# One f32 TanH per decoding step, read twice: its upper half as bf16, the whole of it as f32 weights

## The reference

```python
def step(carry, tgt):
    s, c, alpha = carry
    f = conv(alpha, conv_w)
    e = einsum('a,bta->bt', va, tanh(enc_proj + (s @ Wa_s.T)[:, None, :] + f @ Wa_f.T + ba))
    e = where(mask, e, -1e30)
    alpha_new = softmax(e, axis=1)
    g = einsum('bt,btd->bd', alpha_new, hbatch)
    y = tanh(g @ L_gy_w.T + L_gy_b + s @ L_sy.T) @ L_yy_w.T + L_yy_b
    rec = tgt @ L_ys.T + s @ L_ss.T + g @ L_gs_w.T + L_gs_b
    ig, fg, cg, og = split(rec, 4, axis=1)
    c_next = sig(fg) * c + sig(ig) * tanh(cg)
    s_next = sig(og) * tanh(c_next)
    return (s_next, c_next, alpha_new), y
```

## Time and profile before

| what | us |
|---|---|
| median of 3 runs | 1757.52 |
| the runs | 1752.98, 1757.52, 1757.66 |
| profiled execution, its own time | 1752.67 |
| span of the profiled execution | 1750.9 |
| PE busy | 1652.3 |
| DVE busy | 926.0 |
| ACT busy | 526.4 |
| POOL busy | 385.6 |

### The profile page before, as it was taken

One profiled execution on the slowest core, in us unless ns is written; L12 is line 12 of the kernel. 1 busy time (PEld: TensorE's weight loads), 2 busy tenths in 40 slices (PEclk: granted clock), 3 DMA queues, 4 the chain that ended last, 5 costly groups with the idle time before them and its releaser, 6 DMA issues.

```text
span 1750.9 us, 47280 instructions
## 1 busy us (share of the span) xinstructions
PE 1652.3 (94%) x17747; PEld 960.1 (55%) x17747; DVE 926.0 (53%) x4293; ACT 526.4 (30%) x2023; POOL 385.6 (22%) x1030
## 2 busy tenths in 40 slices
PE   5557999999999999999999999999999999997999
PEld 3444454544555566666666666666666666663443
DVE  5996643331455555555555555555555555553422
ACT  1442230320333333333333333333333333331211
POOL 3334321220000122222222222222222222222311
PEclk8558999999999999999999999999999999997999
DMA  8430000000300000000000000000000000000000
GB/s 323 166 106 8 1 1 0 1 1 9 123 0 0 0 0 0 0 0 0 0 0 0 0 0 0 0 0 0 0 0 0 0 0 0 0 0 1 1 25 25
DMA packets 17363, 34.51 MB, mean 20 GB/s; under 512 B 7476, under 2 KB 8675, under 8 KB 17332
## 3 DMA queue, kind: packets, MB, share of 16 engines
q1 hardware_dynamic: 17332, 34.10, 5.4%
HBM read 32.00 MB, written 2.10 MB: 19 GB/s over the span
## 4 chain that ended last, share of the span: by engine, by line
PE 88%; DVE 8%; issue 2%; POOL 1%; ACT 1%; SPq 1%; DMA 0%; POOLq 0%; DVEq 0%; ACTq 0%
PE bank L1188 27%; PE bank L1073 11%; PE bank L1256 10%; PE bank L1088 6%; PE bank L1232 5%; PE bank L1200 4%; PE bank L1184 4%; PE bank L1206 3%; PE bank L1214 2%; PE bank L1242 2%; PE bank L1219 2%; PE bank L1178 2%; PE bank L1054 1%; DVE xn L559 1%; DVE smax L609 1%
## 5 line engine op out<-in xcount | busy, mean ns | idle before, releaser
L1188 PE MATMUL bank<-krep,identb 128*128 128x512 f16 (+1 forms) x2048 | 604.8, 373 | 0.0
L1256 PE MATMUL bank<-krep,uh 128*128 128x128 f32 x1024 | 215.8, 323 | 0.4 <-DVE krep L764 0.4
L1256 PEld LDWEIGHTS bank<-krep,uh 128*128 128x128 f32 x1024 | 150.0, 188 | 107.8 <-DVE krep L764 91.0
L493 POOL TENSOR_TENSOR sscale<-ex,rinv 128x8 f32 x256 | 50.7, 198 | 645.5 <-DVE rinv L755 645.5
L1188 PEld LDWEIGHTS bank<-krep,identb 128*128 128x128 bf16 x2048 | 171.0, 97 | 8.1
L764 DVE TENSOR_TENSOR krep<-inv,ahn 128x128 f32<-128x128 f32 x512 | 162.3, 356 | 0.0
L1073 PE MATMUL bank<-xT,wbig 128*128 128x512 f16 x672 | 158.2, 387 | 3.6 <-DVE xT L591 3.6
L963 ACT ACTIVATE xs<-gat 64x8 f32<-64x8 f32 x256 | 53.1, 207 | 285.9 <-DVE gat L771 285.9
L743 DVE TENSOR_TENSOR rs<-bank,rin 128x8 f32<-128x8 f32 x256 | 42.7, 167 | 177.5 <-PE bank L1206 177.5
L955 ACT ACTIVATE interT<-bank 128x128 f16<-128x128 f32 x256 | 70.9, 277 | 200.7 <-PE bank L1200 200.7
L1232 PEld LDWEIGHTS bank<-eh,krep 128*128 128x128 f16 x2048 | 67.7, 96 | 102.3 <-ACT eh L960 102.3
(11 more groups left out here) (205 smaller groups left out, 3150.9 us busy)
## 6 DMA issues: line engine op xcount, KB each, us to landing
wbig<-d_gate_qT SPq DMA_DIRECT2D x4, 896.0 KB, 10.0
wbig<-d_up_qT SPq DMA_DIRECT2D x4, 896.0 KB, 20.8
wbig<-d_down_qT SPq DMA_DIRECT2D x1, 3584.0 KB, 30.6
d_out<-x_sb SPq DMA_DIRECT2D x8, 256.0 KB, 2.0
sscale<-d_gate_sT SPq DMA_DIRECT2D x2, 896.0 KB, 8.5
interT<-d_gate_sT SPq DMA_DIRECT2D x2, 896.0 KB, 14.9
sscale<-d_up_sT SPq DMA_DIRECT2D x2, 896.0 KB, 4.2
interT<-d_up_sT SPq DMA_DIRECT2D x2, 896.0 KB, 4.2
```

The source lines that it names most:

```text
L1188: mm(bank[1][:, 0:n], identb[:], hg2[:, 0].rearrange("p h g -> p (h g)")[:, 0:n], start=True, stop=True)
L1256: mm(bank[0][:, 0:P], uh[:, h, :], qv[:, h, :, :], start=False, stop=False, skip_group_check=True)
```

## The change

- ScalarE makes the TanH once, in f32, into `th`, and signals `th_full`. The f16 version and its semaphore are gone.
- The row scores (L1214 before, L1207 after) read `th_top`: the upper 16 bits of each f32 word of `th`, taken as bf16, so every second 16-bit element.
- The column scores are one f32 matmul (L1211 after): `th` as weights, `vae` (8 columns, f32) as moving data. VectorE's subtraction (L746) is gone, and so are the matmul with the remainder (L1222) and its wait.
- The filler ahead of the row scores has 512 columns in place of 384; the filler between L1219 and L1222 is gone. So seven fillers of 512 columns are left.
- In the setup the two VectorE operations that made `vae2` are gone.

```diff
-        vae2 = sb("vae2", [P, 2, 2 * B], F16)
-        th_hi = interT[:, 6, P:P + P // 2].bitcast(F16)
-        th_lo = interT[:, 6, 2 * P:2 * P + P // 2].bitcast(F16)
+        th_top = th.bitcast(BF16).rearrange("p (n two) -> p two n", two=2)[:, 1, :]
...
-            in_halves(vae2[:], vae[:].rearrange("p h b -> p (h b)"))
...
-                    dve.wait_ge(s["th_full"], l + 1)
-                    nc.vector.tensor_tensor(th_lo, th, th_hi, ALU.subtract).then_inc(s["th_lo_ready"], 1)
...
-                    nc.scalar.activation(th_hi, bank[0][:, 0:P], ACT.Tanh).then_inc(s["th_s"], 1)
                     nc.scalar.activation(th, bank[0][:, 0:P], ACT.Tanh).then_inc(s["th_full"], 1)
...
-                    keep_busy(384)
-                    pe.wait_ge(s["th_s"], l + 1)
+                    keep_busy(512)
+                    pe.wait_ge(s["th_full"], l + 1)
                     for b in range(B):
                         for h in range(2):
-                            last = mm(bank[2][b * TH:(b + 1) * TH, h * TH:(h + 1) * TH], vah[:, h, :], th_hi[:, b * TH:(b + 1) * TH],
+                            last = mm(bank[2][b * TH:(b + 1) * TH, h * TH:(h + 1) * TH], vah[:, h, :], th_top[:, b * TH:(b + 1) * TH],
                                       start=False, stop=True, skip_group_check=True)
                     last.then_inc(s["eb_done"], 1)
 
-                    for j in range(2):
-                        mm(bank[3][:, 0:8], th_hi, vae2[:, j, :], start=False, stop=False, skip_group_check=True)
-                    keep_busy(512)
-                    pe.wait_ge(s["th_lo_ready"], l + 1)
-                    mm(bank[3][:, 0:8], th_lo, vae2[:, 0, :], start=False, stop=True, skip_group_check=True).then_inc(s["et_done"], 1)
+                    mm(bank[3][:, 0:8], th, vae[:].rearrange("p h b -> p (h b)"), start=False, stop=True, skip_group_check=True).then_inc(s["et_done"], 1)
 
                     keep_busy(512)
                     keep_busy(512)
```

More of the change, by code:

```diff
@@ L264, in build @@
             vbd_zero setup_v setup_mm setup_cp mask_ready scale_ready
-            pre_done th_s th_full th_lo_ready eb_done et_done mx_ready eh_ready ex_ready el_ready sum_done ah_done hg_done rinv_ready ahn_ready
+            pre_done th_full eb_done et_done mx_ready eh_ready ex_ready el_ready sum_done ah_done hg_done rinv_ready ahn_ready
             prod_ready g_ready q0_ready q1_ready kept tg_ready ab_ready c_ready tc_ready s_ready sh_ready sl_ready sp_done
@@ L1171, in _ @@
             pe.wait_ge(s["rin_ready"], 2 * B)
-            pe.wait_ge(s["part_ready"], 5)
+            pe.wait_ge(s["part_ready"], 4)
             pe.wait_ge(s["identb_ready"], 1)
```

## The result

The changed kernel takes 1760.13 us (median of 20 runs) against 1756.95 us for the one before (20 runs): ratio 1.0021, 95% interval 1.0011 to 1.0031, so 1.9 to 5.4 us slower. The forecast was 1.3 us less. The time lies in the stated range and within 0.3% of the forecast, but it moved the other way, and by more than its interval leaves open. The prediction took 0.3% as the least that such runs can tell; 20 runs of each kernel tell 0.2%.

A forecast was written before the change was run, and what follows sets the result against it. The column scores' path to the exponential was taken to bound each step; 0.05 of filler and 0.39 of f32 matmul nearly replaced it, -0.005 us a step, -1.3 us over 256, giving 1756.2 us, range 1741 to 1768.

The forecast's parts named there:

- the first rival: Filler doesn't hold the row scores' weights: -0.06 us a step, 1742 us; chance 0.15 together with a cheaper f32 matmul.
- Point 1: Filler ahead of the row scores, 384 to 512 columns: their weights load 0.05 us later each step.
- Point 2: Row scores reading every second 16-bit element: no cost, with 0.06 us a step as upper bound.
- Point 3: Column scores' weights can load at 1003.75, which is 1003.70 plus the filler's 0.05 us.
- Point 4: Column scores' f32 matmul, from first load to last end: 0.39 us, with bounds of 0.22 and 0.49.
- the second rival: Column scores' f32 matmul costs more than its columns, full 0.49 us: +0.09 a step, 1780 us; chance 0.12.
- the third: Strided row scores read at half rate: at most +0.06 us a step, 1771 us; chance 0.05.
- Point 6: VectorE's maximum of the row scores: ready at 1004.09, with 0.05 us to spare before the column scores.
- Point 7: Exponential starts at 1004.18 against 1004.19: step changes by -0.005 us, in all -1.3 us.
- Point 8: Step's last two fillers start at 1004.00 to 1004.01, as today, and stay hidden by 0.06 us.
- Point 9: ScalarE free 0.17 us earlier, VectorE 0.29 less to do; both wait there anyway.
- the fourth rival: Granted clock falls with 384 fewer filler columns a step; a twentieth of the steps would cost 19 us; chance 0.04.

The follow-up runs named there:

- b_fill128: The kernel before, with only the filler ahead of the row scores cut from 384 to 128 columns; ratio 1.0004 to the kernel before.
- a_fill384: The kernel after, with the filler ahead of the row scores back at 384 columns in place of 512; ratio 0.9954 to the kernel before.
- b_fill512: The kernel before, with only the filler ahead of the row scores raised from 384 to 512 columns; ratio 1.0081 to the kernel before.
- a_one_fill256: The kernel after, with one semaphore for the exponential's wait and 256 filler columns ahead of the row scores in place of 512; ratio 0.9842 to the kernel before.
- a_onesem: The kernel after, with the column scores' and the maximum's signals on one semaphore, so ScalarE has one wait; ratio 0.9983 to the kernel before.
- a_fill128: The kernel after, with the filler ahead of the row scores cut from 512 to 128 columns; ratio 0.9873 to the kernel before.
- a_one_tail256: The kernel after, with one semaphore, 128 filler columns ahead of the row scores and the step's last filler at 256 instead of 512; ratio 0.9842 to before.
- a_one_nofill: The kernel after, with one semaphore for the exponential's wait and all fillers out of the loop; 1801.6 us, ratio 1.0282 to the kernel before.
- a_max32: The kernel after, with the maximum taken over 32 of the 64 row scores only; ratio 0.9979 to the kernel before.
- a_swap: The kernel after, with ScalarE's two waits ahead of the exponential in the other order; ratio 1.0089 to the kernel before.

## Why the prediction was wrong, point by point

- *What bounds the kernel before*: it is right that the column scores, over the second TanH and the subtraction, are last (b_fill128). It is wrong on what is next: "The maximum of the row scores is done at 1003.84 + 0.23 = 1004.07 and has 0.09 us to spare". With 0.094 from the maximum to ScalarE it had 0.034 to spare, the 1.046 of the table less 0.390 + 0.622.
- *What holds the row scores*: right. The filler does, with 0.09 behind its streaming (a_fill384, b_fill512, a_one_fill256), and the first rival fell with it. In the Trainium skill the rule of TensorEngine Tiling (Array Packing), Key Properties, that changing the mode drains the engine, is what these three agree with.
- *Point 1*, +0.05: measured 0.054. *Point 2*, strided reading, 0: the eight matmuls take 0.23 in both kernels. *Point 3*: 0.165 behind, as before. *Point 4*, 0.39 taken from rows with 64, 128 and 16 columns: measured 0.39. With these the second rival (0.49) and the third (strided reading) fell.
- *Point 5*: the column scores end at 0.999 after the TanH's start, before at 1.007, forecast 0.99 to 1.00. Right.
- **Point 6 is the step that failed.** It gave the maximum's path two hops of 0.04, the hop seen at other places, and found 0.05 to spare. Measured were 0.068 from the row scores' end to VectorE, which stood at 1003.77 and 1003.84 in the earlier trace rows and was put down to the subtraction ("no longer behind the subtraction"), though it is the same without one; and 0.094 to ScalarE, which no row of before could show, since there the maximum was not last. Together 0.08 was missing, so the path came 0.027 behind that of the column scores instead of 0.05 ahead. The longer hop to ScalarE is that of the semaphore instruction: a_onesem takes it away, and the step falls from 4.449 to 4.416, below the 4.426 of before. That the forecast time was still within 0.3% is no merit of the mechanism: most of the missing 0.08 was swallowed by the 0.05 that the path was thought to spare.
- *Point 7*, -0.005 a step: measured in the profiles +0.021 for the distance from TanH to exponential and +0.023 for the step. With the sizes found the sum would be 0.444 + 0.622 = 1.066 against 1.046, so +0.020, and 256 x 0.020 = 5 us.
- *Point 8*: the last two fillers start 0.24 behind the f32 matmul's first load, within 0.02 of the forecast, and stay hidden. *Point 9*: right, 49 us of VectorE and 43 us of ScalarE gone for nothing.
- *The clock* stayed at 1.00 in the loop, so the fourth rival didn't come. It fell in kernels with fewer filler columns still: once in a_fill128, six times in a_one_tail256, throughout in a_one_nofill.
- One case beside the first rival, a cheap f32 matmul, had the maximum last, but with the same short hops, so at 1004.13 and faster. No rival had it last with the f32 matmul at 0.39, and none had a hop of another length.
- What is open: the sizes say 5 us, the profiled loops 5.9, the runs 3.7 (1.9 to 5.4). I can't say where the difference lies. a_max32 and a_onesem, too, came out 1.4 and 0.5 us faster in the runs than by their steps (3.7 against 2.3, 3.0 against 2.5), inside their intervals; a_swap came out slower than by its steps.

## What to carry to other kernels

Filler matmuls are free only as long as they have streamed before the signal behind them comes, and where the shape of the weights changes behind a filler, the 0.09 us that pass before the next load must fit in too. So the length of a filler must be chosen by the time of the signal and not by what was saved elsewhere. When a chain is cut, work out the path that stood second with its own measured hops, and not with those of other instructions: a wait for two semaphores can cost more on one side than on the other (0.094 to 0.097 against 0.04 here), and the order of the waits in the code decides which. The signal expected last belongs on the instruction itself, which here is the wait written first, and one shared semaphore avoids the question.

## What was not expected of the hardware

- Where ScalarE waits for two semaphores, it starts 0.094 to 0.097 us behind the signal that the separate wait instruction takes (after, a_swap) and 0.037 to 0.040 behind the other (before, a_max32, b_fill512); with one semaphore 0.037 (a_onesem).
- The maximum on VectorE starts 0.068 behind the end of the eight matmuls with 32-column weights, with the subtraction ahead of it (before) and without it (after). Behind matmuls with 128-column weights VectorE starts after 0.038 (the reciprocal of `rinv`, median of before and of after). What makes the difference is not shown.
- An idle engine's releaser in the profile is the event that ended last, and not always the one that held: it named the TanH where the filler held (after, 0.23 idle), and the column scores where the maximum held.
- With all fillers out the granted clock stood at 0.50 in a stretch of 1178 us (a_one_nofill). With 256 of the 3200 filler columns of a step cut it fell six times, for 3.4 to 6.8 us, in the one execution profiled (a_one_tail256).
